# Gated delta rule with a routed feed-forward block: where the gate projections of the last head stand

## The reference

```
q, k, v, z = xn @ W_qkvz        (per key head: 128 + 128 + 256 + 256 channels)
q, k, v = silu(causal convolution with 4 taps);  q, k l2-normalised
per chunk: T = inverse of a unit lower triangular matrix (k k' scaled by decays and beta)
scan over chunks: v' = T (v*beta - k_decayed @ state);  out = q @ state + (q k') @ v'
                  state = state * decay + k' @ v'
x = out * silu(z);  x = x * rsqrt(mean(x*x) + eps) * norm_weight
result = x @ W_out
```

## Time and profile before

| | |
|---|---|
| time, median of 3 runs | 1593.17 us (1590.95 to 1595.19) |
| profiled execution, its own time | 1593.2 us |
| its span | 1591.4 us |
| TensorE busy | 1529.3 us, 96% of the span |
| VectorE busy | 1115.5 us, 70% |
| ScalarE busy | 777.2 us, 49% |
| GpSimd busy | 442.6 us, 28% |
| mean granted TensorE clock | 0.982 of full speed |
| the four gate calls of head 15 | within 1495.35 to 1511.13 us |
| iteration 15 (the last scan) | from 1553.47 us to the end |

### The profile page before, as it was taken

How to read it: one execution, slowest core, us unless ns; L and a number is a source line. 1 busy time by engine, 2 the same in 40 slices (tenths; PEclk the granted TensorE clock), 3 DMA queues, 4 the chain that set the end, 5 groups by cost and what they waited for, 6 DMA issues and landing times.

```text
span 1591.4 us, 29140 instructions
## 1 busy us (share of the span) xinstructions
PE 1529.3 (96%) x10922; PEld 1078.1 (68%) x10922; DVE 1115.5 (70%) x2447; ACT 777.2 (49%) x1672; POOL 442.6 (28%) x279
## 2 busy tenths in 40 slices
PE   6999999999989995899999999999999999999987
PEld 4767666666647773667767767767767767766756
DVE  5455354554483326688988988988888888888874
ACT  3443444435423332464564664664664664664641
POOL 1000000014051004243643543544443343343310
PEclk9999999999999998899999999999999999999998
DMA  4343451222413324223324314414314314313200
GB/s 131 96 146 114 144 172 54 67 76 99 143 65 116 107 83 116 71 61 102 88 52 103 89 50 104 104 33 105 93 31 93 92 33 92 91 44 81 58 18 27
DMA packets 225051, 136.88 MB, mean 86 GB/s; under 512 B 160976, under 2 KB 196304, under 8 KB 224912
## 3 DMA queue, kind: packets, MB, share of 16 engines
q1 hardware_dynamic: 221840, 126.62, 29.4%
q0 software_dynamic: 3072, 8.39, 1.7%
HBM read 94.85 MB, written 35.91 MB: 82 GB/s over the span
## 4 chain that ended last, share of the span: by engine, by line
PE 89%; DVE 4%; issue 2%; SPq 1%; DMA 1%; POOL 1%; ACT 1%; POOLq 0%; DVEq 0%; ACTq 0%
PE ps L860 7%; PE ps L759 7%; PE ps L527 7%; PE ps L778 7%; PE ps L622 4%; PE ps L552 4%; PE ps L993 4%; PE ps L656 3%; PE ps L799 3%; PE ps L542 3%; PE ps L830 3%; PE ps L704 3%; PE ps L694 3%; PE ps L1016 3%; PE ps L809 2%
## 5 line engine op out<-in xcount | busy, mean ns | idle before, releaser
L1300 ACT ACTIVATE vs<-ps 128x256 f32<-128x256 f32 x128 | 49.1, 383 | 261.0 <-PE ps L799 256.7
L2140 POOL TENSOR_TENSOR qg<-qT,Ebc 128x1024 f32<-128x1024 f32 x32 | 74.8, 2361 | 356.9 <-PE ps L830 356.9
L759 PE MATMUL ps<-xnT,gv 128*128 128x512 f32 x256 | 121.5, 618 | 12.5 <-DVE cv L1765 12.0
L1765 DVE SCALAR_TENSOR_TENSOR cv<-ps,cw,cv 128x1022 f32<-128x1022 f32 (+2 forms) x96 | 122.6, 1279 | 14.0 <-ACT cv L1247 10.1
L860 PE MATMUL ps<-wout,xT 128*128 128x256 f32 x512 | 128.9, 396 | 2.2 <-DVE total L1875 2.2
L778 PE MATMUL ps<-xnT,gz 128*128 128x512 f32 x256 | 124.2, 610 | 3.2 <-DMA gz<-in_gz 2.9
L1776 DVE SCALAR_TENSOR_TENSOR cv<-ps,cw,cv 128x1022 f32<-128x1022 f32 (+2 forms) x96 | 122.6, 1277 | 6.3 <-ACT cv L1279 4.0
L1875 DVE SCALAR_TENSOR_TENSOR total<-ps,rr,total 128x256 f32<-128x256 f32 x256 | 118.9, 481 | 9.9 <-POOL rr L2146 3.0
L527 PE MATMUL ps<-xrT,cv 128*128 128x512 f32 x256 | 117.8, 593 | 1.1 <-ACT xrT L1144 0.8
L1207 ACT ACTIVATE we<-ps,bias 128x128 f32<-128x128 f32 (+3 forms) x128 | 65.7, 525 | 98.2 <-DVE bias L1585 98.2
L860 PEld LDWEIGHTS ps<-wout,xT 128*128 128x128 f32 x512 | 93.2, 192 | 28.3 <-issue 12.6
(11 more groups left out here) (255 smaller groups left out, 3575.7 us busy)
## 6 DMA issues: line engine op xcount, KB each, us to landing
xs_dram<-zeros SPq DMA_DIRECT2D x16, 1024.0 KB, 7.6
dec<-grow_dram SPq DMA_DIRECT2D x32, 512.0 KB, 4.7
Ebc<-erow_dram SPq DMA_DIRECT2D x32, 512.0 KB, 5.1
cv<-in_wqk SPq DMA_DIRECT2D x16, 512.0 KB, 3.6
xn<-xs_dram SPq DMA_DIRECT2D x47, 128.0 KB, 2.0
ys_dram<-yg SPq DMA_DIRECT2D x47, 128.0 KB, 1.9
we<-in_we SPq DMA_DIRECT2D x16, 352.0 KB
cv<-in_wv SPq DMA_DIRECT2D x16, 256.0 KB, 3.6
```

The source lines that it names most:

```text
L759: last = mm(ps[:, (Y, X)[r] + b, :], gv[:, k, r * D:(r + 1) * D], xnT[:, k, b * S:(b + 1) * S], start=(k == 0), stop=(k == HK - 1))
L1765: ins = stt(row, pair(bank)[:, :, 0:S - k], cw[:, f, i, TAPS - 1 - k:TAPS - k], row, ALU.mult, ALU.add)
L2140: tt(qg[:, r], qT[:], Ebc[:, r], ALU.mult).then_inc(fl["g_qg"], 1)
```

## The change

For head 15 alone, the four gate projections and the two silus are moved from iteration 14 to iteration 15. On TensorE, (0, 0) now stands behind `solved` of step 0 of the last scan, (0, 1) behind `key_state` into step 1, and (1, 0) and (1, 1) together behind `solved` of step 1, ahead of `new_state` of step 1. On ScalarE both silus stand behind the deltas of step 1. Two waits are changed to fit: the value projection of head 15 with r = 1, which writes the same banks, waits for `v_M` (the product with the decays that reads these banks) in place of the silu; the first gate call also waits for `v_vs` (the scaled values, read from these banks). All other heads are as before.

```diff
@@ project_values(n, r), n == NK - 1, r == 1
-                    pe.wait_ge(fl["a_sz"], 2 * n + 2)
+                    pe.wait_ge(fl["v_M"], 2 * n + 2)
@@ project_gates(n, r, b)
+                if b == 0 and r == 0 and n == NK - 1:
+                    pe.wait_ge(fl["v_vs"], n + 1)
@@ TensorE, loop of the heads
                         solved(h, 0, b)
-                if middle:
+                if middle and n < NK - 1:
                     project_gates(n, 0, 0)
+                if h == NK - 1:
+                    project_gates(h, 0, 0)
...
                         key_state(h, 1, b)
-                if middle:
+                if middle and n < NK - 1:
                     project_gates(n, 0, 1)
+                if h == NK - 1:
+                    project_gates(h, 0, 1)
                 if scan:
                     for b in range(B):
                         solved(h, 1, b)
                 if middle:
                     turn_keys(n)
+                if h == NK - 1:
+                    for b in range(B):
+                        project_gates(h, 1, b)
                 if scan:
                     for b in range(B):
                         new_state(h, 1, b)
...
-                if middle:
+                if middle and n < NK - 1:
                     project_gates(n, 1, 0)
...
-                if middle:
+                if middle and n < NK - 1:
                     project_gates(n, 1, 1)
@@ ScalarE, loop of the heads
                         deltas(h, 1, b)
-                if middle:
+                if h == NK - 1:
+                    for r in range(R):
+                        gate_silu(h, r)
+                if middle and n < NK - 1:
                     gate_silu(n, 0)
+                if middle:
                     decayed_keys(n, 0)
...
-                if middle:
+                if middle and n < NK - 1:
                     gate_silu(n, 1)
```

More of the change, by code:

```diff
@@ L1420, in _ @@
                         deltas(h, 1, b)
+                if h == NK - 1:
+                    for r in range(R):
+                        gate_silu(h, r)
+                if middle and n < NK - 1:
+                    gate_silu(n, 0)
                 if middle:
-                    gate_silu(n, 0)
                     decayed_keys(n, 0)
```

## The result

The changed kernel takes 1599.33 us in the median of 11 runs (1597.12 to 1600.78), the kernel before 1593.7 us (1590.95 to 1595.29, 11 runs). The ratio is 1.0034, with a 95% interval of 1.0025 to 1.0043, so it is 5.6 us slower. No execution of the one kernel overlaps the other's: the fastest of the changed kernel took 1597.12 us, the slowest of the kernel before 1595.29. The prediction was 1600.0 us. Three slow executions in the comparisons further down, of 2788, 3173 and 5537 us, are left out of every ratio.

What follows compares the result with a forecast made beforehand. It took scan step, VectorE's inverse and DMA to bound iteration 14's first half, and TensorE the nearly full last scan. Terms -2.6 + 1.3 + 8.1 = +6.8 us on 1593.2 gave 1600.0 us, range 1594.3 to 1603.5.

Steps and rivals of the forecast that it cites:

- TensorE does not set iteration 14: Iteration 14's first half: scan step, VectorE's inverse and DMA bound it, so shedding 6.9 us of TensorE work saves 2.6 us.
- just in time: Iteration 14, DMA needed by `solve_start`: lands at 1503.6 us against a start at 1503.65, so TensorE changes gain no more there.
- The table load lands in front of the values' silu and is paid in full: Iteration 14, line 1284: the Silu table load moves to the values' silu, fully exposed, giving 1.3 us back.
- The case with a drain beside it: Iteration 14's table load: by the skill page a drain of some 1.38 us comes on top, an estimated 2.7 us.
- The last scan hides nothing but its small gaps: Last scan up to `new_state` of step 1: 6.9 us of gate matmuls plus 1.9 stall, less 0.7 of gaps, 8.1 us.
- The stall for the silu: Last scan, calls (1, 0) and (1, 1): TensorE waits for ScalarE's silu of r = 0, a new stall of 1.9 us.
- the prediction let the clock fall for as long as before: Start of the last scan: half clock lasting to 1559.4 us adds 3.0 us behind 1553.47, leaving 0.7 us of gaps.
- Iteration 14 getting shorter by all 6.9 us: Rival, iteration 14: it gains everything TensorE sheds, 6.9 us, so 1594.4 us in all; chance 0.12.
- The last scan hiding the work: Rival, last scan: bound by ScalarE and VectorE, it hides the moved matmuls, 1591.9 us or less; chance 0.05.
- A further fall of the clock behind the stall: Rival, last scan: the 1.9 us stall brings the clock down once more, 2.6 us more, 1602.5 us; chance 0.15.
- The clock making up for everything: Rival: without the earlier kernel's three clock falls the 6.8 us are made up, 1593.1 us, not slower; chance 0.10.

Runs made afterwards that it cites:

- e1: The changed kernel with head 15's gate projections and silus left out, gating with stale values; 1611.94 us against 1612.86 for the kernel before, ratio 0.9993.
- e2: The changed kernel plus a one-column Silu behind the deltas of step 1 of iteration 14; 1616.24 us against 1612.86 for the kernel before, ratio 1.0027.
- e3: The changed kernel with the r = 1 gate calls behind `key_state` into step 2, their silu behind step 2's deltas; ratio to the kernel before 1.0038.
- e5: The changed kernel with both r = 0 gate calls in the last scan issued twice; 1620.81 us against 1612.93 for the kernel before, ratio 1.0058.
- e8: The changed kernel with the silu of r = 0 ahead of step 1's deltas on ScalarE; 1598.4 us against 1594.74 for the kernel before, ratio 1.0023.
- e9: The changed kernel with both the early one-column Silu (e2) and the earlier r = 0 silu (e8); 1596.86 us against 1594.74 for the kernel before, ratio 1.0015.
- e7: The kernel before plus a one-column Exp behind step 3's deltas in iteration 14, forcing a table load; 1614.02 us against 1612.93, ratio 1.0009.
- e4: The kernel before with head 15's r = 1 gate calls moved into iteration 14's wait for the blocks; 1609.43 us against 1612.86, ratio 0.9982.
- e6: The kernel before with e4's move, and call (0, 1) behind `key_state` into step 2 of iteration 14; 1608.62 us against 1612.93, ratio 0.9978.

## Why the prediction was right, point by point

- **TensorE does not set iteration 14.** Right, shown by the changed kernel's trace and by e1. Predicted were 2.6 us up to `first_blocks`; the changed kernel has 2.0, and e1, e2, e3, e5, e8 and e9 have 2.3 to 2.5 (33.0 to 33.2 us behind `MT`). The missing 0.5 us in the changed kernel's trace is the DMA of the blocks. The prediction called it just in time, issued at 8.5 us behind `MT` and landed 2.8 us later; here it was issued at 9.1 us and took 2.9, and VectorE waited 0.48 us for it. In the six experiments it was issued at 8.3 to 8.7 us, so the half microsecond is one of that execution; the change does not always bring it. In those VectorE starts the inverse 11.5 to 11.6 us behind `MT`, close to the 11.4 predicted.
- **The table load lands in front of the values' silu and is paid in full.** Right: 1.29 us more of waiting at line 766, gone with e2, brought about alone with e7. The case with a drain beside it (2.7 us) is ruled out for this place by the wait in e7, 1.72 us instead of 3.1.
- **The last scan hides nothing but its small gaps.** Right in kind, shown by e5. In size: predicted 8.1 us, in the two profiled executions 14.72 - 8.09 = 6.6 us. Two terms were off. The stall for the silu was 1.39 us and not 1.9. The silu started 1.37 us after `solved` and not 1.65, since the deltas started after 0.64 us and took 0.83, where the earlier trace rows gave 0.75 and 0.90; and the idle time counts from the end of a `solved` of 1.05 us, where the sum took 0.89. Second, the prediction let the clock fall for as long as before, 6.8 us; it fell for 3.4, which is worth 1.3 us; nothing in the prediction foresaw that. With the clock taken out, 13.03 us (e2) stand against some 5.3 us (from `new_state` of step 1 to that of step 2 there are 5.33 us in the kernel before), 7.7 us added.
- **The rivals.** Iteration 14 getting shorter by all 6.9 us is refuted by e1. The last scan hiding the work is refuted by e5. A further fall of the clock behind the stall did not come in the changed kernel's trace, nor in those of e2 and e5, which have the same stall of 1.39 us. The clock making up for everything did not come in any of the 11 executions of the changed kernel, the fastest of which is slower than the slowest of the kernel before. But the clock is worth more than the prediction's spread around its sum suggests: in the eleven traces the start of the last scan has none, 3.4 or 6.8 us at half clock, which moves a single execution by up to 3 us, half of the effect sought. The profiled execution of e2, without a fall there, took 1610.87 us, less than the median of the kernel before; from the first `MT` to the end it has 99.72 us, only 0.6 more than the kernel before with its three falls.
- **The sum.** -0.9 us up to the last scan (predicted -1.3), +6.6 (predicted +8.1), -0.2 behind it (the next step takes 5.17 us instead of 5.33): +5.5 us, predicted +6.8. The errors have opposite signs in part. That the median came out within 0.7 us of the forecast is partly luck: the difference was 5.6 us and not 6.8, and the kernel before ran at 1593.7 us, 0.5 above the base of the sum.

Left open: what sets the moment at which the clock falls, and with it how long the fall lasts; no run was made to vary that moment alone. What the eleven traces show of it stands in the last section.

## What to carry to other kernels

A late stretch that looks idle has to be read for who is idle: here the last scan had gaps of 0.3 us on the engine that was to take the work, while the iteration in front of it had one wait of 5.3 us for a DMA. Filling that wait (e4) made the kernel faster by 0.18% with the same matmuls. When the first use of an activation function moved, the table load went to the next instruction that needed the table, and that one was on the chain; an instruction of 0.20 us put ahead of it took the load off the chain again (e2). And when a moved result has several readers, follow each through to the buffer that it frees.

## What was not expected of the hardware

- The granted clock falls for stretches of 3.4 us or 6.8 us, in nearly the same kernel: the fall behind the wait for `T11BD` took 6.8 us in the kernel before, the changed one, e3, e5 and e7, and 3.4 us in e1, e2, e8 and e9, after waits of 5.1 to 5.4 us in all nine. The length goes with the moment: the falls of 6.8 us began 2.0 to 3.1 us before `first_blocks`, those of 3.4 us 0.1 to 0.7 us before it. At the last scan it is alike: the one fall of 6.8 us (the kernel before) began 0.9 us ahead of the first operation, the six of 3.4 us began 0.6 to 1.5 us behind it, and in e2, e3, e5 and e9 none came, behind the same wait of 1.49 us. With the wait for `T11BD` cut to 1.71 us (e4) and 1.90 us (e6) no fall came there.
- The pair of `deltas` on ScalarE takes 0.83 us and starts 0.64 us after a `solved` that TensorE reached without a gap (1562.82 us in the changed kernel); behind one that had waited for the residuals (1560.37 us in the kernel before) it takes 0.90 us and starts after 0.75 us.
